# A four-layer attention kernel: one pool of PSUM banks, row-tiled transposes of the probabilities, the residual kept with features on partitions, and new order tables

## What is computed

```python
# layer 0: 16 heads of 64
q, k, v = x @ Wq, ctx @ Wk, ctx @ Wv                  # 1024 wide each
logits = q . k / 8 + col_bias                         # 64 x 64 per head
x = softmax(logits) @ v @ Wo + bo + x
# layers 1 to 3: 16 query heads of 8, 4 key/value heads of 8
xn = x * rsqrt(mean(x * x) + 1e-5) * norm_w
q, k, v = xn @ wq, ctx @ wk, ctx @ wv                 # q 128 wide, k and v 32 wide
x = x + softmax(q . k / sqrt(8)) @ v @ wo
```

## Time and profile before

| what | value |
|---|---|
| median of 3 runs | 1443.73 us (1443.47 to 1444.94) |
| the profiled execution | span 1442.6 us |
| PE / PEld busy | 1416.4 us (98%) / 1151.5 us (80%) |
| DVE / ACT / POOL busy | 1090.9 / 1043.0 / 787.3 us (76 / 72 / 55%) |
| granted TensorE clock | 0.999 of 2.4 GHz |

### The profile page before, as it was taken

The page is one execution under the profiler, slowest core; times in us unless marked ns, Lnnn a source line. Parts: engine busy times, 40 slices in busy tenths (PEclk is TensorE's granted clock), DMA queues, the critical chain, the costliest instruction groups (busy, mean ns, idle before and its releaser), DMA issues.

```text
span 1442.6 us, 56878 instructions
## 1 busy us (share of the span) xinstructions
PE 1416.4 (98%) x23692; PEld 1151.5 (80%) x23692; DVE 1090.9 (76%) x2281; ACT 1043.0 (72%) x2321; POOL 787.3 (55%) x905
## 2 busy tenths in 40 slices
PE   8999999999999999999999999999999999999987
PEld 6778878888888888788888788888888887888765
DVE  1557777777777777777778777777777777777887
ACT  3567776777777777767777777777777777677777
POOL 3445555545555455555455555455554555554687
PEclk9999999999999999999999999999999999999999
DMA  5010111010111001111001110101110001110000
GB/s 157 21 28 18 29 29 30 24 29 18 30 29 31 23 18 29 30 29 30 24 19 29 29 30 24 29 19 29 29 32 23 23 25 30 29 28 18 18 7 14
DMA packets 58540, 41.16 MB, mean 29 GB/s; under 512 B 17456, under 2 KB 54064, under 8 KB 58288
## 3 DMA queue, kind: packets, MB, share of 16 engines
q1 hardware_dynamic: 57872, 37.19, 9.9%
q10 hardware_dynamic: 416, 0.33, 0.1%
HBM read 20.68 MB, written 4.19 MB: 17 GB/s over the span
## 4 chain that ended last, share of the span: by engine, by line
PE 96%; ACT 1%; DVE 1%; POOL 1%; issue 1%; DMA 0%
PE bank L706 17%; PE bank L694 16%; PE bank L753 16%; PE bank L771 8%; PE bank L721 7%; PE scores L743 7%; PE bank L790 7%; PE scores L732 5%; PE bank L762 5%; PE bank L796 3%; PE bank L777 3%; PE bank L713 2%; PE bank L665 1%; ACT E L863 1%; DVE st L954 0%
## 5 line engine op out<-in xcount | busy, mean ns | idle before, releaser
L644 POOL TENSOR_TENSOR E<-E,st 128x512 f32<-128x512 f32 x512 | 530.2, 1044 | 535.7 <-DVE st L966 535.5
L963 DVE TENSOR_REDUCE st<-E 128x8 f32<-128x512 f32 x512 | 344.7, 675 | 81.0 <-ACT E L859 40.0
L863 ACT COPY E<-bank 128x512 f32<-128x512 f32 x512 | 298.1, 598 | 96.7 <-PE bank L753 95.5
L859 ACT ACTIVATE E<-E,inv 128x512 f32<-128x512 f32 x384 | 278.5, 734 | 57.2 <-DVE E L958 56.7
L954 DVE TENSOR_REDUCE st<-scores 128x8 f32<-128x512 f32 x372 | 244.0, 683 | 97.0 <-PE scores L743 97.0
L753 PE MATMUL bank<-ident,E 128*128 128x128 f32 x2048 | 301.5, 276 | 0.9 <-POOL E L644 0.7
L753 PEld LDWEIGHTS bank<-ident,E 128*128 128x128 f32 x2048 | 241.5, 141 | 69.3 <-issue 28.2
L706 PE MATMUL bank<-wv,cT 128*128 128x374 f32 (+1 forms) x768 | 271.4, 478 | 0.0
L694 PE MATMUL bank<-cT,wk 128*128 128x256 f32 x1024 | 245.9, 384 | 7.0 <-issue 5.9
L958 DVE TENSOR_TENSOR E<-scores,st 128x512 f32<-128x512 f32 x372 | 245.9, 669 | 0.1
L694 PEld LDWEIGHTS bank<-cT,wk 128*128 128x128 f32 x1024 | 188.9, 192 | 32.1 <-issue 6.3
(11 more groups left out here) (58 smaller groups left out, 1627.0 us busy)
## 6 DMA issues: line engine op xcount, KB each, us to landing
KB<-K SPq DMA_DIRECT2D x1536, 8.0 KB
cT<-in_ctx_t SPq DMA_DIRECT2D x32, 256.0 KB, 2.8
xq<-in_x_t SPq DMA_DIRECT2D x32, 128.0 KB, 2.2
xin<-in_x SPq DMA_DIRECT2D x32, 128.0 KB, 2.3
out<-xN SPq DMA_DIRECT2D x30, 128.0 KB, 1.9
wk<-in_L_xattn_Wk SPq DMA_DIRECT2D x3, 256.0 KB, 5.5
wv<-in_L_xattn_Wv SPq DMA_DIRECT2D x2, 374.0 KB, 6.4
wq<-in_L_xattn_Wq SPq DMA_DIRECT2D x1, 512.0 KB, 6.2
```

Of the source, the lines that this page charges most:

```text
L644: e.tensor_tensor(E3, E3, wide(stat[s][u][:, 16:24]), ALU.mult).then_inc(g_nrm.sem, 1)
L859: e.activation(E[s][u][:, :], E[s][u][:, :], ACT.Exp, scale=inv[s][:, u // 2:u // 2 + 1]).then_inc(a_exp.sem, 1)
L863: e.copy(E[s][u][:, :], bank_of["t", g, l, u][:, :]).then_inc(a_et.sem, 1)
L963: e.tensor_reduce(stat[s][u][:, 8:16], heads(E[s][u][:, :]), AX, ALU.add).then_inc(d_sum.sem, 1)
```

## The change

- **One PSUM pool.** All eight banks form one tensor `psum`. A step takes the banks that, by the tables' times of the evicting steps (`DUE`), come free first; `s` of layers 1 to 3 takes two pairs of adjacent banks.
- **Transposes in row tiles.** A `t` step covers two units. Each 128 x 128 block is done as two transposes of 64 rows, on rows 0 to 63 and 64 to 127 of the array, each with 64 moving columns, into two different banks. `pv0` and `pv` index the new layout.
- **Residual with features on partitions.** `wo0` and `wo` have the weights `wo0`/`wos` stationary and 256 tokens moving; DVE writes `xT` directly (one instruction adds `bo` and the input `xq`). `q` follows it at once. PE transposes `xT` for the squares (`x2`), which ACT reads from PSUM. `xt`, its ACT copy, `xin`, its DMAs and POOL's addition of `bo` are gone. The output is stored with features first.
- **Tables anew**, with slots of their own for groups 0 to 2 and 28 to 31; `PERIOD` is 41.834682 in place of 43.53, and the repeated semaphore waits ahead of `k` (`PE_FILL`, L690) are removed.

```diff
-PE_FILL = (18, 18, 16, 16)
-PERIOD = 43.53
+PERIOD = 41.834682
-    "t": {0: (94.04, 91.9, 96.41, 97.28),
+    "t": {0: (275.01196, 275.0097), 1: (316.76559, 316.76407), 2: (358.56335, 358.55832), 3: (358.73538, 358.73502)},
...
-        scores = ctx.enter_context(nc.psum_tensor("scores", [128, 4, 512], F32))
-        banks = [ctx.enter_context(nc.psum_tensor(f"bank{i}", [128, 512], F32)) for i in range(4)]
+        psum = ctx.enter_context(nc.psum_tensor("psum", [128, 8, 512], F32))
...
+        held, free = [[]] * 8, [float("-inf")] * 8
+        for st in of(PE_ORDER, *ON_ACT, *ON_DVE, "s", "t"):
             _, g, l, u = st
+            evictors = held_until(st)
+            if st[0] == "s" and l > 0:
+                at = min(([i, i + 1, j, j + 1] for i in range(5) for j in range(i + 2, 7)),
+                         key=lambda four: max(free[i] for i in four))
+            else:
+                at = sorted(sorted(range(8), key=lambda i: free[i])[:len(evictors)])
+            bank_of[st] = at
             before[st] = [ev for i in at for ev in held[i]]
+            for i, evs in zip(at, evictors):
+                held[i], free[i] = evs, max(DUE[ev] for ev in evs)
...
                 if kind == "k":
                     w.wait_ge(l_c[g % NC], g)
                     w.wait_ge(l_wk[u], u)
-                    for _ in range(PE_FILL[u]):
-                        e.wait_ge(l_wk[u].sem, 16)
...
                 elif kind == "t":
                     w.wait_ge(l_ident, "ident")
-                    w.wait_ge(g_nrm, ("nrm", g, l, u))
-                    for k in range(4):
-                        m = e.transpose(bank[:, 128 * k:128 * k + 128], E[s][u][:, 128 * k:128 * k + 128], ident[:, :])
+                    w.wait_ge(g_nrm, ("nrm", g, l, 2 * u), ("nrm", g, l, 2 * u + 1))
+                    for r in range(2):
+                        for k in range(4):
+                            for i in range(2):
+                                rows, c = slice(64 * i, 64 * i + 64), 256 * r + 64 * k
+                                m = e.transpose(psum[:, at[i], c:c + 64], E[s][2 * u + r][rows, 128 * k:128 * k + 128],
+                                                ident[rows, rows])
...
                 elif kind == "wo0":
-                    for p in halves(g, u):
-                        for j in range(8):
-                            m = e.matmul(bank[:, 128 * p:128 * p + 128], QT[s][:, j, 128 * p:128 * p + 128],
-                                         wo0[:, j, :], start=(j == 0), stop=(j == 7))
+                    for j in range(8):
+                        m = e.matmul(bank[:, tokens], wo0[:, j, :], QT[s][:, j, tokens], start=(j == 0), stop=(j == 7))
...
                 elif kind == "q":
-                    w.wait_ge(a_ev, ("xt", g, l, u))
+                    w.wait_ge(d_ev, ("wo0" if l == 1 else "wo", g, l - 1, u))
...
-                elif kind == "xt":
+                elif kind == "x2":
+                    w.wait_ge(l_ident, "ident")
                     w.wait_ge(d_ev, ("wo0" if l == 1 else "wo", g, l - 1, u))
                     for p in halves(g, u):
-                        to_rows(bank, 128 * p, xN[s][:, p, :], p == halves(g, u)[-1])
+                        m = e.transpose(bank[:, 128 * p:128 * p + 128], xT[s][:, 128 * p:128 * p + 128], ident[:, :])
...
                 elif kind == "wo":
-                    for p in halves(g, u):
-                        m = e.matmul(bank[:, 128 * p:128 * p + 128], QT[s][:, 1, 128 * p:128 * p + 128],
-                                     wos[:, l - 1, :], start=True, stop=True)
+                    m = e.matmul(bank[:, tokens], wos[:, l - 1, :], QT[s][:, 1, tokens], start=True, stop=True)
...
                 elif kind == "et":
+                    w.wait_ge(p_t, ("t", g, l, u // 2))
+                    e.copy(E[s][u][:, :], psum[:, bank_of["t", g, l, u // 2][u % 2], :]).then_inc(a_et.sem, 1)
...
-                    e.tensor_tensor(flat(xN[s])[:, tokens], bank[:, tokens], flat(xin[s])[:, tokens], ALU.add
-                                    ).then_inc(d_ev.sem, 1)
+                    e.scalar_tensor_tensor(xT[s][:, tokens], bank[:, tokens], bo[:, 0:1], xq[g % NX][:, tokens], ALU.add,
+                                           ALU.add).then_inc(d_ev.sem, 1)
```

More of the change, by code:

```diff
@@ L59 @@
 }
 ACT_TIME = {
[L61 to L72, removed]
@@ L81 @@
[L81 to L92, removed]
@@ new lines @@
+    "sum": {0: (297.02151, 295.44202, 298.23236, 295.4855),
+            1: (330.29544, 325.2821, 324.67969, 322.99854),
+            2: (355.92682, 357.64319, 353.22229, 353.84384),
+            3: (385.63016, 387.93042, 385.70099, 386.80649)},
+    "rcp": {0: (297.31781, 300.05978, 299.30844, 295.61166),
+            1: (332.24454, 329.2522, 327.79468, 325.21655),
+            2: (356.38431, 359.26358, 353.9884, 356.17328),
+            3: (386.52185, 389.64825, 387.58481, 386.84079)},
+    "wo0": {0: (311.81454,)},
@@ L448, in xattn_kernel @@
         powers = sb("powers", [128, 2, NP])
-        xin = [sb(f"xin{s}", [128, NP, C]) for s in range(NS)]
         xq = [sb(f"xq{i}", [128, T]) for i in range(NX)]
-        xN = [sb(f"xN{s}", [128, NP, C]) for s in range(NS)]
         xT = [sb(f"xT{s}", [128, T]) for s in range(NS)]
@@ new lines, in xattn_kernel @@
+            bank_of[st] = at
+            before[st] = [ev for i in at for ev in held[i]]
+            for i, evs in zip(at, evictors):
+                held[i], free[i] = evs, max(DUE[ev] for ev in evs)
+            if st[0] == "s" and l == 0:
+                for r in range(2):
+                    scores_of[g, l, 2 * u + r] = psum[:, at[r], :]
+            elif st[0] == "s":
+                for p in halves(g, u):
+                    for r in range(2):
+                        scores_of[g, l, 2 * p + r] = psum[:, at[2 * r]:at[2 * r] + 2, 256 * p:256 * p + 256].rearrange(
+                            "p r (h k) -> p r h k", k=64)
@@ L520, in xattn_kernel @@
         l_b = signal("l_b", range(7), 16)
-        l_x = [signal(f"l_x{s}", range(s, NG, NS), 16) for s in range(NS)]
         l_xq = [signal(f"l_xq{i}", range(i, NG, NX), 16) for i in range(NX)]
@@ L578, in sync_program @@
                 e.dma_start(xq[i][:, :], t["x_t"][i]).then_inc(l_xq[i].sem, 16)
-            for s in range(NS):
-                e.dma_start(xin[s][:, :, :], x_r[s]).then_inc(l_x[s].sem, 16)
             for i, n in enumerate("AB"):
@@ L599, in sync_program @@
                     w.wait_ge(p_ev, *[("q0", g, 0, i) for i in range(4)])
+                    w.wait_ge(d_ev, *[("wo0", g, 0, part(g, p)) for p in range(NP)])
                     e.dma_start(xq[g % NX][:, :], t["x_t"][g + NX]).then_inc(l_xq[g % NX].sem, 16)
@@ L731, in tensor_program @@
                                     lo, n, j, c = 64 * h2, 128 * u + 64 * b2, 2 * jj + par, 128 * jj + 64 * b2
-                                    m = e.matmul(scores[64 * par:64 * par + 64, bank[h2], c:c + 64],
+                                    m = e.matmul(psum[64 * par:64 * par + 64, at[h2], c:c + 64],
                                                  QT[s][lo:lo + 64, j, n:n + 64], KTg[lo:lo + 64, j, n:n + 64],
@@ L742, in tensor_program @@
                                 lo, b = 32 * r, 2 * p + b2
-                                m = e.matmul(scores[64 * b2:64 * b2 + 64, bank[r], 256 * p:256 * p + 256],
+                                m = e.matmul(psum[64 * b2:64 * b2 + 64, at[r], 256 * p:256 * p + 256],
                                              QT[s][lo:lo + 32, 0, 64 * b:64 * b + 64],
```

794 lines of the change are left out of this document (513 added, 281 removed), and 77 rows, old and new, of tables (ACT_ENDS, PE_ENDS).

## The result

The changed kernel takes 1450.05 us (median of 5 runs, 1448.09 to 1450.73), the one before 1443.77 us beside it. The ratio is 1.0039 (95% interval 1.0027 to 1.0052): slower by 0.4%, about twice what a measurement of this kernel can tell from no change, where the prediction said 1383 us and at most 1402. The profiled execution spans 1448.9 us.

A forecast was written before the change was run, and what follows sets the result against it. PE's issued work was taken as the bound for 91% of the span. Terms -103.6 + 40.6 - 4.9 + 3 + 4 = -60.9 us took the profiled 1442.6 to 1381.7 us, 1383 us timed; range 1367 to 1402.

The forecast's parts named there:

- A steady group of 41.9 us: One steady group on PE, `wo0` to `wo0`, would go from 43.84 to 41.9 us.
- Set of two row tiles, 58.5 ns: In `t`, 2048 sets at 58.5 ns replace full transposes at 109 ns, saving 103.6 us.
- Rival B: Inside `t`, the two row tiles do not halve the set: at 109 ns a set, timed 1482 us; chance 0.07.
- A change of tile shape, 0.165 us: On PE, 246 more switches of tile shape at 0.165 us each, costing 40.6 us.
- I book 0.1 us a group: Between `wo0` and the `q` that needs its residual, PE would wait 0.1 us a group, +3 us.
- Waits removed ahead of `k`: Removing the repeated semaphore waits on PE's sequencer ahead of `k` would cost and gain nothing.
- Rival C: In the steady part PE waits for DVE, POOL or a bank: 1402 to 1440 us; chance 0.12.
- The ends, +4 us and +-6: Transpose savings in the last 68 us may not show, +4 us; each layer's chain there is even, +-6 us.

The follow-up runs named there:

- the kernel at place 140: Changed kernel with the fourth `q0` moved between `wo` and `q`, plus padding in groups 4 to 25 fixing `wo0`'s fourth matmul at place 140 of 256: 1415.78 us.
- the two last edits: On the kernel at place 140: one `xq` load put ahead of the key rearranging, 1413.53 us; then also eight single steps moved in groups 24 to 31, 1410.65 us.

## Why the prediction was wrong, point by point

The pieces of PE's work that I had priced by rows were nearly right, and the time between them was wrong.

- **A steady group of 41.9 us: right.** With the waits out of the way it takes 42.03, 4 us over the run more than predicted. Where nothing stands in the way, the sum of PE's pieces holds.
- **Set of two row tiles, 58.5 ns: nearly.** 32 records of two `t` take 1.21 us in the timeline of the changed kernel (the row below), the last lasting about 0.23 of it: 15.5 distances in 0.98, 63 ns. That is 9 us over 2048 sets. Rival B was wrong: two loads of 140 ns go with each set of 63 ns, so the loads do not set its pace. My reason, some 60 ns of occupation in a load of 141 ns, no row shows. The Trainium skill, "TensorE: Matmul & The Clock Gate", LDWEIGHTS, says that a load's time goes by its columns and not by its rows. In this the trace agrees, 140 ns for 64 rows and 141 for 128, and still the rival did not come about.
- **A change of tile shape, 0.165 us: right in kind.** `pv`, two `t`, `wo` in the rows below: 1.03 + 1.14 + 0.63 (chain) against 16 x 0.055 + 16 x 0.063 + 0.43 = 2.32 plain; 0.48 over for three changes, 0.16.

The rows of the changed kernel for these two points: the timeline of two `t`,

```profile
589.63 1.21 PE L958 MATMUL psum<-ident,E 64*128 64x64 f32 x32
```

the group of their loads (busy us, mean ns),

```profile
L958 PEld LDWEIGHTS psum<-ident,E 64*128 64x128 f32 x4096 | 146.3, 140 | 58.0 <-issue 35.5 <-ACT QT L1050 9.4 <-DVE E L1155 2.9
```

and the chain:

```profile
588.67 1.03 PE psum L996 x64
589.70 1.14 PE psum L958 x32
590.84 0.63 PE psum L1001 x2
```

- **"I book 0.1 us a group" between `wo0` and `q`: failed.** The place was named rightly, the wait is 0.31 us there, and what it sets off was left out: moving one step behind `wo0` gave 22.5 us instead of 3. The wait itself was misread by 0.2 us. I took 443.64, where the chain puts the end of `wo0`, as the start of the next work too, but PE begins that while the last record of `wo0` still runs, in the timeline of the kernel before at 443.48:

```profile
443.48 0.71 PE L753 MATMUL bank<-ident,E 128*128 128x128 f32 x5
```

So `wo` would have left PE free at 443.91, with the sum ready at 444.10, or 444.17 at the 0.49 us that the new addition takes. Then I priced the wait as if only PE felt it. Late `q` makes late `s`, and the steps behind it are in a fixed order: 0.31 us at `q` became 0.87 us a group.
- **"Waits removed ahead of `k` ... cost and gain nothing ... an error here is a gain": failed.** In the kernel before their removal costs 41 us, the widest miss of any step. In the changed kernel, which lacks them too, the stalls inside steps are 12.5 us, and with `q0` moved taking them away gave 11.7. I had asked what the waits hide behind, and not what their number does.
- **Rival C (waits in the steady part): right that waits would come, with 36.8 us more of idle time in the middle, partly wrong in cause and wrong in chance.** I gave it 0.12, since eight banks give room and DVE had time to spare. DVE has time to spare still (74%). The wait behind `wo0` is for DVE, as C allows, but since the sum comes too late for the order and not since DVE falls behind; the stalls of the blocks C did not have.
- **The ends, +4 us and +-6: too small.** In the kernel at place 140 PE idles 31 us after 1150 us, before 16, and the granted clock of the last 65 us is 0.79 (before, 0.97 in its last 68; the changed kernel 0.85 in its last 74). With the load's late issue (4 us between 150 and 200 us) this is some 19 us, of which the two last edits brought back about 5. How much is the order and how much the drain of the last groups stays open.

In one sum: 1383 + 4 (group) + 22.5 (`q` behind `wo0`) + 11.7 (blocks) + 19 (load and ends) comes to 1440 of 1450; the rest, 10 us, I can't place. A part may be the clock: in the kernel at place 140 PE is busy for 29 us at the lower level of 1.2 GHz, before for 3. What this costs is not shown.

## What to carry to other kernels

When PE is the bound and a change makes its work shorter, price each wait that the shorter work uncovers with its followers, and before judging the change try one step of independent work between the result and the step that waits for it: here one constant decided between slower and 1.3% faster. Count TensorE's instructions in a repeated stretch. If it is a multiple of 256, any edit that adds or drops an instruction is a second change, to be tested by itself. If it isn't, the sign is a stall inside a step with no releaser, always at the same number modulo 256 and 1.1 to 1.6 us after the end of a q8 transfer. Aligning the stretch so that no block holds only quick tiled instructions took these stalls away in one order here and a third of them in another, so count them again afterwards.

## What the runs showed of the hardware

- TensorE's instructions come in blocks of 256, one q8 transfer of 16.4 KB each (192 transfers for 49,176 instructions before, 198 for 50,706 after, 187 for 48,088 without `PE_FILL`). The first instruction of a block began 1.14 us or more after the end of its transfer in all 1523 cases that were counted, and 1.14 to 1.61 us after it in the 116 that stalled. A transfer took 0.9 to 1.5 us and started, in the median, 0.8 us after the block ahead had begun. Blocks of 3.3 us and less stalled often but not always; longer ones stalled where the transfer started late, and why it does is open. All these stalls lie inside steps, most of them in tiled ones.
- A jump over up to 211 instruction places, ahead of a matmul record of 216 ns among others like it, cost nothing that shows: a steady group with it takes 42.03 us, the groups without stalls and without it 42.04.
- A transpose in a 64 x 128 tile: load 140 ns, as long as that of a full one (141), and 63 ns for a set of two.
- SP's issues of small copies take 0.62 us each and come every 0.67 us; 16 of them ahead of a load take 10.7 us of the queue.
- The granted clock is lower at the end, where PE idles: 0.88 from 1350 to 1400 us and 0.78 after, where the kernel before had 1.00 and 0.97.

```profile
1350.00:1400.00 50.00, 41.51 (x986) 33.26 (x986) 42.23 (x95) 37.28 (x83) 35.32 (x43) 0.88 0.06 13
1400.00:1449.00 49.00, 33.91 (x715) 25.33 (x713) 31.31 (x71) 32.43 (x78) 32.65 (x43) 0.78 0.05 13
```
